# A two-stage recurrent layer and mixture of experts on one core: the order of work between the chunk loop and the expert slots

## The reference, cut to what matters

```python
x = x + layernorm(attn(layernorm(x)))      # attn: k, v, r projections, scan, Wo; then channel mixing
xf = layernorm(x)
shared = (gelu(xf @ w1s) * (xf @ w2s)) @ w3s
idx = argmax(xf @ Wg)                      # one of 8 experts for each token
for e in range(8):
    y = (gelu(xf @ W1[e]) * (xf @ W2[e])) @ W3[e]
    final = final + where(idx == e, y, 0)
x = x + layernorm(shared + final)
```

## Time and profile before

| | us |
|---|---|
| median of 3 runs | 1024.32 (1023.39 to 1027.34) |
| the profiled execution's own time | 1025.26 |
| its span, first to last instruction | 1023.5 |
| PE busy | 932.7 |
| DVE busy | 719.4 |
| POOL busy | 587.9 |
| ACT busy | 587.0 |

### The profile page before, as it was taken

How to read it: one execution, slowest core, us unless ns; L and a number is a source line. 1 busy time by engine, 2 the same in 40 slices (tenths; PEclk the granted TensorE clock), 3 DMA queues, 4 the chain that set the end, 5 groups by cost and what they waited for, 6 DMA issues and landing times.

```text
span 1023.5 us, 28050 instructions
## 1 busy us (share of the span) xinstructions
PE 932.7 (91%) x9734; PEld 839.7 (82%) x9734; DVE 719.4 (70%) x1653; ACT 587.0 (57%) x1014; POOL 587.9 (57%) x800
## 2 busy tenths in 40 slices
PE   2387899999999999999999999779999999999994
PEld 1266789888888888888888878568999999999994
DVE  6988898998998998998998984513444444444442
ACT  5477677778768868868868755223333333333331
POOL 5446567767766766866866542434445554545553
PEclk9688999999999999999999999889999999999998
DMA  7113151351352252152161268375886788476510
GB/s 236 62 53 112 44 185 50 118 206 34 113 208 56 88 205 81 63 212 96 41 231 68 84 206 285 135 238 194 289 263 216 238 271 261 154 257 195 183 54 22
DMA packets 87338, 156.36 MB, mean 153 GB/s; under 512 B 5549, under 2 KB 68142, under 8 KB 82160
## 3 DMA queue, kind: packets, MB, share of 16 engines
q1 hardware_dynamic: 35760, 72.74, 20.8%
q10 hardware_dynamic: 46960, 65.89, 19.9%
q0 software_dynamic: 4560, 16.98, 4.3%
HBM read 178.35 MB, written 50.51 MB: 224 GB/s over the span
## 4 chain that ended last, share of the span: by engine, by line
PE 60%; DVE 17%; issue 8%; ACTq 6%; ACT 4%; POOL 2%; DMA 2%; DVEq 0%; POOLq 0%
PE up L342 12%; PE up L344 12%; PE up L343 12%; PE yp L342 6%; PE yp L343 6%; PE yp L344 6%; DVE er L1084 5%; PE yp L562 3%; ACTq L881 2%; DVE mixed L1012 2%; PE tp L351 1%; DVE arena L983 1%; DVE val L1099 1%; ACTq L901 1%; ACTq L884 1%
## 5 line engine op out<-in xcount | busy, mean ns | idle before, releaser
L342 PE MATMUL up<-mix_s,arena 128*128 128x128 f16 x1248 | 211.2, 219 | 3.6 <-DVE ex L1426 2.1
L343 PE MATMUL up<-mix_s,arena 128*128 128x128 f16 x1248 | 211.1, 219 | 0.0
L344 PE MATMUL up<-mix_s,arena 128*128 128x128 f16 x1248 | 211.1, 219 | 0.0
L342 PE MATMUL up<-xf_s,arena 128*128 128x256 f16 x512 | 140.3, 274 | 3.4 <-issue 2.4
L1655 POOL TENSOR_TENSOR kf_s<-ex,kf_s 128x512 f16<-128x512 f32 x78 | 90.2, 1156 | 88.5 <-ACT kf_s L942 88.4
L343 PE MATMUL up<-xf_s,arena 128*128 128x256 f16 x512 | 140.4, 274 | 0.0
L344 PE MATMUL up<-xf_s,arena 128*128 128x256 f16 x512 | 140.3, 274 | 0.0
L1426 DVE SCALAR_TENSOR_TENSOR ex<-up,ex 128x512 f32<-128x512 f32 x78 | 53.9, 691 | 105.0 <-ACT ex L936 104.7
L342 PEld LDWEIGHTS up<-mix_s,arena 128*128 128x128 f16 x1248 | 122.1, 98 | 5.3 <-DVE ex L1426 3.4
L343 PEld LDWEIGHTS up<-mix_s,arena 128*128 128x128 f16 x1248 | 122.1, 98 | 0.4
L344 PEld LDWEIGHTS up<-mix_s,arena 128*128 128x128 f16 x1248 | 122.1, 98 | 0.0
(11 more groups left out here) (228 smaller groups left out, 2893.8 us busy)
## 6 DMA issues: line engine op xcount, KB each, us to landing
arena<-w_split ACTq DMA_DIRECT2D x117, 1024.0 KB
arena<-in_W SPq DMA_DIRECT2D x24, 1024.0 KB, 6.2
w_split<-arena SPq DMA_DIRECT2D x24, 1024.0 KB, 9.1
rows<-routed_rows ACTq DMA_DIRECT2D x39, 261.0 KB, 2.9
routed_rows<-x_in SPq DMA_DIRECT2D x8, 650.0 KB, 6.3
normed<-routed_rows ACTq DMA_DIRECT2D x39, 128.0 KB, 2.5
x_in<-in_x SPq DMA_DIRECT2D x16, 256.0 KB, 2.8
x_res<-in_x SPq DMA_DIRECT2D x16, 256.0 KB, 2.8
```

The costliest lines, as they stand in the source:

```text
L342: pe.matmul(out, stat(0), mov(0), start=first, stop=False)
L343: pe.matmul(out, stat(0), mov(1), start=False, stop=False)
L344: return pe.matmul(out, stat(1), mov(0), start=False, stop=last)
```

## The change

It moves instructions and adds no arithmetic. By part:

- **Every step, PE:** `shared_gate(2)` goes from behind `output` to in front of it. `shared_down`'s last piece is cut in two of four f each.
- **Every step, DVE:** `halo` of the next chunk goes from in front of `gate` (and of the weight piece of `own(0)`) to behind it.
- **Step 16:** PE's pieces of chunk 13 go in front of `ranks` and `transpose_normed2`; DVE's `shared(3)` in front of `x1_sum`; POOL's `sh_lo(3)` in front of `inverse3`; chunk 15's `transpose_xf` and `xf_hi` go from step 17 into step 16's end, between the two halves of chunk 14's second token tile.
- **Step 17:** DVE's `shared(0)` and `shared(1)` go within the slot table's computation; the loads of slots 0 and 1 go from ACT to SP (`first_slots`), in front of `zeros_at_ends`.
- **Slots:** PE's wait for `y_sh` goes from in front of slot step 0 to slot step 2's down product.

```diff
--- before.py
+++ after.py
@@ -312,6 +312,26 @@
                     at = sp.value_load(end_at[0:1, e:e + 1], min_val=0, max_val=E * REGION - P)
                     sp.dma_start(routed_rows[bass.ds(at, P), 0:ID], zero_rest).then_inc(S("zeroed_rest"), 16)
 
+            def first_slots():
+
+                sp.wait_ge(S("slot_table"), 2)
+                sp.wait_ge(S("scattered_xf"), 16 * TT)
+                for b in range(2):
+                    sp.wait_ge(S(f"scattered{b}"), 16 * TT * (NC // 2 - b))
+                for m in range(3):
+                    sp.wait_ge(S(f"expert_out{m}"), 16 * E)
+                for n in range(2):
+                    at = sp.value_load(slot_row[0:1, n:n + 1], min_val=0, max_val=E * REGION - P)
+                    sp.dma_start(slot_x[n], routed_rows[bass.ds(at, P), XF:XF + C]).then_inc(S(f"slot_x_in{n}"), 16)
+                    e = sp.value_load(slot_expert[0:1, n:n + 1], min_val=0, max_val=E - 1)
+                    for part in range(2):
+                        def half(w):
+                            return w.rearrange("p m h (k n) -> p (m h k) n",
+                                               k=CT)[:, :, part * F // 2:(part + 1) * F // 2]
+                        sp.dma_start(half(expert_w[n][:, 0:2]),
+                                     half(w_split[bass.ds(e, 1), :, 0:2].rearrange("e p m h n -> (e p) m h n"))
+                                     ).then_inc(S(f"slot_w{part}_{n}"), 16)
+
             def step(i, p, h):
                 for part in range(2):
                     for n in own_pieces(OWN_LOADS, i, part):
@@ -329,6 +349,7 @@
                 for e, m in early_piece(i, p, h) + last_late(i, p, h) + late_now(i, p, h):
                     store_expert(e, m)
                 if at_step(i, NC + 1):
+                    first_slots()
                     zeros_at_ends()
 
             chunk_steps(sp, step)
@@ -393,6 +414,8 @@
                     wait(pe, S(f"slot_w2_{1 - b}"), 16 * (h + b))
                     wait(pe, S("slot_h_lo"), 2 * j)
                     wait(pe, S("slot_sum"), j - 2)
+                    if at_step(j, 2):
+                        pe.wait_ge(S("y_sh"), NC)
                     for f in range(FT):
                         mm = three(pe, yp[1 - b][:, 0, :], lambda s: slot_h[1 - b][:, s, f, :],
                                    lambda s: expert_w[1 - b][:, 2, s, f * C:(f + 1) * C], f == 0, f == FT - 1)
@@ -426,11 +449,11 @@
                         wait(pe, S("xnT"), CT * (c0 + 1) if on(c0) else CT * NC)
                         transposes(tp[1], normed2, "t2_mm")
 
-                def transpose_xf():
-                    if on(c2):
-                        wait(pe, S("xf"), TT * (c2 + 1))
-                        wait(pe, S("placed"), c2)
-                        transposes(tp[0], rows[p][:, :, XF:XF + C], "t4_mm")
+                def transpose_xf(c, b):
+                    if on(c):
+                        wait(pe, S("xf"), TT * (c + 1))
+                        wait(pe, S("placed"), c)
+                        transposes(tp[0], rows[b][:, :, XF:XF + C], "t4_mm")
 
                 def transpose_next():
                     if on(i + 1):
@@ -572,25 +595,30 @@
                         wait(pe, S("x3a"), c + 2 if not at_step(c, NC - 1) else NC)
                     if q < PAIRS:
                         wait(pe, S("sh_lo"), PAIRS * c + q + 1)
-                    for f in (2 * q, 2 * q + 1) if q < PAIRS else range(FT):
-                        t = q // PAIRS
+                    t = q // PAIRS
+                    parts = ((0, FT // 2), (FT // 2, FT))
+                    for f in (2 * q, 2 * q + 1) if q < PAIRS else range(*parts[q - PAIRS]):
                         m = three(pe, yp[1][:, t, :], lambda s: sh_s[:, s, f, t * P:(t + 1) * P],
                                   lambda s: shared_w[:, 2, s, f * C:(f + 1) * C], f == 0, f == FT - 1)
-                    if q == PAIRS:
+                    if q == PAIRS + 1:
                         m.then_inc(S("sh_dn_mm"), 1)
 
                 before = c3 if not at_step(i, NC + 1) else -1
                 projection(0)
                 projection(1)
-                transpose_normed2()
-                ranks(before)
-                projection(2)
-                shared_down(before, 0)
-                shared_down(before, 1)
-                shared_down(before, 2)
-                shared_down(before, 3)
-                transpose_xf()
-                shared_down(before, 4)
+                if not at_step(i, NC):
+                    transpose_normed2()
+                    ranks(before)
+                    projection(2)
+                for q in range(PAIRS):
+                    shared_down(before, q)
+                if at_step(i, NC):
+                    ranks(before)
+                    transpose_normed2()
+                if not at_step(i, NC + 1):
+                    transpose_xf(c2, p)
+                shared_down(before, PAIRS)
+                shared_down(before, PAIRS + 1)
                 if at_step(i, NC + 1):
                     gate()
                     shared_gate(0)
@@ -611,8 +639,8 @@
                     ranks(c2)
                 for q in range(4):
                     channel_mix_down(q)
+                shared_gate(2)
                 output()
-                shared_gate(2)
                 shared_up(2)
                 shared_gate(3)
                 shared_up(3)
@@ -620,12 +648,13 @@
                     pe.wait_ge(S("placed"), NC)
                     slot_step(-1, 1, -1)
                 if at_step(i, NC) or at_step(i, NC + 1):
-                    for q in range(PAIRS + 1):
+                    for q in range(PAIRS + 2):
+                        if at_step(i, NC) and q == PAIRS + 1:
+                            transpose_xf(c1, 1 - p)
                         shared_down(c2, q)
 
             chunk_steps(pe, step)
 
-            pe.wait_ge(S("y_sh"), NC)
             slot_steps(pe, slot_step, 0)
 
 
@@ -729,10 +758,10 @@
                     if on(i + 1):
                         channel_norm(xnT[1 - p], tp[1], G1, B1, i + 1, "t0_mm", "xnT", "mix", 3, "halo")
 
-                def xf_hi():
-                    if on(c2):
-                        wait(act, S("t4_mm"), c2 + 1)
-                        wait(act, S("sh_up_mm"), PAIRS * c2)
+                def xf_hi(c):
+                    if on(c):
+                        wait(act, S("t4_mm"), c + 1)
+                        wait(act, S("sh_up_mm"), PAIRS * c)
                         act.activation(xf_s[:, 0], tp[0][:], ACT.Copy).then_inc(S("xf_hi"), 1)
 
                 def mix2_hi(m):
@@ -825,7 +854,8 @@
                 if not at_step(i, NC + 1):
                     xf(c2, p)
                 above(0)
-                xf_hi()
+                if not at_step(i, NC + 1):
+                    xf_hi(c2)
                 above(1)
                 mix2_hi(1)
                 mix2_hi(0)
@@ -853,8 +883,6 @@
                 sh_hi(0)
                 mix_hi(1)
                 sh_hi(1)
-                if at_step(i, NC + 1):
-                    first_slot()
                 late_hi()
                 early_hi()
                 mix_hi(2)
@@ -870,12 +898,11 @@
                 sh_hi(3)
                 if at_step(i, NC):
                     xf(c1, 1 - p)
+                    xf_hi(c1)
                 if at_step(i, NC + 1):
                     slot_step(-1, 1, -1)
                 if last:
                     y_shared(c2, p, h - 1)
-                if at_step(i, NC + 1):
-                    second_slot()
 
             def expert_of(n):
                 return act.value_load(slot_expert[0:1, bass.ds(n, 1)], min_val=0, max_val=E - 1)
@@ -903,24 +930,6 @@
             def load_x(n, b):
 
                 act.dma_start(slot_x[b], routed_rows[rows_of(n), XF:XF + C]).then_inc(S(f"slot_x_in{b}"), 16)
-
-            def first_slot():
-
-
-                act.wait_ge(S("slot_table"), 2)
-                act.wait_ge(S("scattered_xf"), 16 * TT)
-                act.wait_ge(S("scattered0"), 16 * TT * (NC // 2))
-                act.wait_ge(S("scattered1"), 16 * TT * (NC // 2 - 1))
-                load_x(0, 0)
-                for m in range(3):
-                    act.wait_ge(S(f"expert_out{m}"), 16 * E)
-                for part in range(2):
-                    load_weights(0, 0, part, "sh_up_mm", PAIRS * NC - 2)
-                load_x(1, 1)
-
-            def second_slot():
-                for part in range(2):
-                    load_weights(1, 1, part, "sh_up_mm", PAIRS * NC)
 
             def slot_step(j, b, h):
                 if is_slot(j + 1):
@@ -1259,7 +1268,9 @@
                     dve.tensor_copy(end_at[:], next_row[:, 0, :]).then_inc(S("end_at"), 1)
                     parts()
                     slots_of_experts()
+                    shared(0)
                     places_of_slots()
+                    shared(1)
                     last_slots()
                 else:
```

(23 more changed lines are left out.)

## The result

| | before | changed |
|---|---|---|
| median of the runs, us (range; runs) | 1024.26 (1022.42 to 1027.34; 14) | 1017.64 (1013.10 to 1019.86; 14) |
| ratio, 95% interval | | 0.9932, 0.9919 to 0.9945 |
| profiled span, us | 1023.5 | 1017.2 |

The change makes the kernel 6.6 us faster, 0.7%. The forecast was 1007.5, a gain of 16.8: the direction is right, the size is not, and the time lies above the forecast range of 997 to 1016.

A forecast was written before the change was run, and what follows sets the result against it. PE was taken to bound the chunk loop. Gains of 7.6 (loop), 4.0 (step 2) and 5.2 (passage) sum to 16.8 us, taking the profiled 1025.26 to 1008.5; with the median 0.94 lower, forecast 1007.5, range 997 to 1016.

The forecast's parts named there:

- Loop, steps 3 to 14 and step 2: Chunk loop: PE's waits for the output projection's `rw` vanish, winning 7.6 us in steps 3 to 14 and 4.0 in step 2.
- The rival by which the later projection holds up the next step: Loop: `transpose_normed2` waits as long as the projection did, the 7.6 us are lost, time 1015; chance 0.10.
- `rw` comes 1.6 earlier: Loop, DVE: choosing experts before the halo copy fills an idle of 1.86 us, so `rw` comes 1.6 us earlier.
- the gate's 1.3 us: Loop, PE: the shared gate puts another 12 matmuls, 1.3 us, in front of the output projection.
- Head of step 16: Start of step 16: later transposes delay DVE's mixing and the lo half of xf, a loss of 1.0 us (0 to 2).
- End of step 16: Earlier lo half 3 lets the gate multiply at 652.2 instead of 658.42: 6.2 us won, the head's 1.0 paid.
- The five short jobs: End of step 16: POOL's root, ACT's scaling, PE's transposes and xf's two halves, 0.5 to 1.2 each, together 4.9 us.
- Step 17: Earlier table and loads on SP: PE's slot 1 transposes start at 671.5 instead of 684.85, 13.4 us ahead.
- 2.1 MB at 340 GB/s take 6.2: Step 17: slot 1's row, queued behind slot 0's weights on SP, comes near 671.3.
- The slots: First slots: zeros behind loads hold ACT; PE waits 7.7 us before slot 2's up product, plus 1.6 for lower clock.
- The rival by which the zeros don't bind: First slots: zeros land before 682, PE reaches slot 2 at 686.4 to 688, time about 1000; chance 0.27.
- 5.2 for the passage: Steps 16 and 17 through slot 2's up product: 5.2 us won, 0.8 at the lower transfer rate, 8.5 at the higher.

The follow-up runs named there:

- the loop edits alone: Kernel before plus only the third shared gate ahead of the output projection and the choice of experts ahead of the halo copy: 1012.20 us, 0.9883.
- the old head back: Changed kernel with PE's normed2 transposes, ranks and third projection again ahead of chunk 13's pieces: 1010.93 us; with zero writes also ahead of first loads: 1007.12.
- the best kernel here: Changed kernel with zeros before loads, PE's old step 16 order, last down products before slot 0's transposes, DVE's split waiting for POOL's root: 1004.17 us, 0.9811.
- gate alone: Kernel before with only the third shared gate moved ahead of the output projection: 1011.89 us, 0.9872.
- the old head with the zeros first: Changed kernel with PE's old order at the start of step 16 and SP's zero writes ahead of the first slots' loads: 1007.12 us, 0.9852.
- rows first: The best kernel here with both slots' rows loaded ahead of the weights on SP: 1006.11 us, 0.9818.
- table whole with late zeros: Changed kernel with PE's old step 16 order and both shared products behind the slot table, zeros still behind the loads: 1009.53 us, 0.9851.

## Why the forecast was right in sign and wrong in size

- **Loop, steps 3 to 14 and step 2** (7.6 + 4.0): right, 11.3 us by the profile, 11.1 by the medians of the loop edits alone. The rival by which the later projection holds up the next step is out: 0.5 us of waits for `normed` in all. The share of the two edits was wrong: the gate does it all. "`rw` comes 1.6 earlier" took the idle of step 12 for that of every step and left out POOL beside `num` (1.53 instead of 0.69). That the sum held all the same is owed to the gate's 1.3 us, which cover even the longest wait (1.0) alone.
- **Head of step 16** (forecast -1.0, measured -3.9 in its stretch; the old head back gains 4.0 and 5.5 there). **This is the step that failed first:** the forecast followed the late transposes through DVE's mixing to the lo half of `xf` alone. That path came as forecast (11.5 us into the step; the forecast says 11.3, its own terms give 11.7). It left out the path through ACT, on which the scaling of chunk 14's rows stands behind the norm of normed2: PE waited 2.09 us for it, and the lower clock behind it cost about 2 more, so the gate started at 14.3. The move of one PE instruction pushed back another chain that PE needs a microsecond later.
- **End of step 16** (forecast +7.2, measured +3.1). Lo half 3 came as forecast: POOL ends it at 638.93, 3.6 us behind the start of the last down products (forecast 647.3 - 643.7 = 3.6). The five short jobs behind it were priced at 4.9 from durations of each engine alone; they took 9.0 (638.93 to 647.93). The root's last operation ran beside DVE's split (1.87 instead of 0.20), x1, which the root waits for, ran beside the two lo halves and ended only at 639.21, and PE's last 12 matmuls ahead of the gate ran at the lower clock.
- **Step 17** (forecast +7.2, measured +1.7). The table was priced at its old length plus two products, 9.3; it took 11.5, so slot 0's row made PE wait 3.2 instead of 1.2. The larger miss is slot 1's row: "2.1 MB at 340 GB/s take 6.2" had PE's transposes of slot 1 6.8 us behind those of slot 0; they came 10.2 behind (662.49 to 672.65). 353 and 361 GB/s were moved from 665 to 675, but only 180 from 660 to 665. Of the 5.4 us short in this stretch 2.1 are the table's and 3.4 this row's. The last down products between them, 8.1 us instead of 5.3 as 25 of 48 matmuls ran at the lower clock, cost nothing: PE waited 1.62 for the row behind them.
- **The slots** (forecast -8.2, measured -5.4). The mechanism is right: the zeros land late, ACT stands at `zeroed_rest`, and PE waits ahead of slot 2's up product and then runs at the lower clock. From SP's first load on, ACT was free again after 28.2 us (forecast 27.5), and PE began slot 1's transposes after 12.4 (forecast 9.3). So the wait was 4.65 instead of 7.7 mostly because PE came there later itself: the smaller loss here is the other side of step 17's miss, not a better term. The lower clock behind the wait cost 1.5 (forecast 1.6). The rival by which the zeros don't bind is out.
- **Range.** Its upper end, 1016, took in one rival, the loop's; the passage's own terms were given no downside together, though two of them rest on chains of short jobs whose sum was taken from undisturbed durations. 5.2 for the passage had a lower bound of 0.8, and the runs gave -5.

Open: what the 1 to 3 us are that the old head gains by the ratios beyond its own stretch, how much time the interleaved table costs, and what decides which of DVE and POOL starts first at x1.

## What to carry to other kernels

Where an instruction is moved behind a late one, follow what stands behind it on each engine that it releases, also the work that belongs to another chain; the price is there. A small operation on a critical chain that meets a large one of the engine beside it can take the large one's time: a short wait in the large one's stream can be worth microseconds. Where the same bytes must arrive in the same gap, reordering the queue moves the wait; look at the DMA share before trying, and keep of a combined change only the parts that pay (the best kernel here leaves the new head of step 16 out).

## What was not expected of the hardware

- Operations of DVE and POOL stretch side by side: POOL's 128x2 operation 0.20 to 1.87 us; DVE's 128x273 product 0.43 to 1.94; a cast of 128x39 0.17 to 1.14; the pair x1 0.91 (at 596.06) to 1.78 or 2.74.
- The same idle of 2.39 to 2.40 us ahead of step 16's transposes was followed by 24 matmuls of which 13 to 16 ran at the lower clock (4.1 to 4.5 us for the 24) in five kernels (before, gate alone, the old head with the zeros first, rows first, table whole with late zeros), and all at the upper (2.78 us) in six others. PE's timeline, first of the loop edits alone, then of the old head with the zeros first:

```profile
600.29 0.66 PE L351 MATMUL tp<-ident,normed 128*128 128x128 f32 x4 [2.39 <-ACT normed L669]
...
601.07 0.27 PE L343 MATMUL yp<-arena,sh_s 128*128 128x256 f16 x1
```

```profile
599.24 0.66 PE L372 MATMUL tp<-ident,normed 128*128 128x128 f32 x4 [2.40 <-ACT normed L694]
...
600.08 0.42 PE L364 MATMUL yp<-arena,sh_s 128*128 128x256 f16 x1
```

  Some 1.6 us between two profiles can come from this alone, and none of these runs says what decides it.
- Eight writes of zeros took SP 8.4 to 9.4 us to issue ahead of the first slots' loads on its queue or without them, and 13.3 to 14.9 in the three kernels in which they stand behind 4 MB of them: the issuing engine itself is held, not only the landing.
